# Expert thresholds found in two shares of sixteen experts, the second inside the loop of experts

## The reference, cut to what matters

```python
Sm = softmax(xf @ W_router + b_router)           # 8192 tokens x 32 experts
G_ek, idx_ek = jax.lax.top_k(Sm.T, 256)          # for each expert
tokens = xf[idx_ek]
up = einsum(tokens, W_up[group]) + b_up          # 128 -> 341, one W_up for 4 experts
Eout = einsum(silu(up), W_down[e]) + b_down      # 341 -> 128
y = zeros.at[idx_ek].add(G_ek[..., None] * Eout)
h = h + y
```

## Time and profile before

| what | value |
|---|---|
| median of 3 runs | 1282.54 us (1282.24 to 1286.24) |
| the profiled execution, its time | 1287.31 us |
| the profiled execution, its span | 1285.5 us |
| PE busy, DVE, ACT, POOL | 1072.1, 829.3, 677.6, 736.3 us |
| mean granted TensorE clock | 0.930 of full speed |
| chain that ended last: POOL, issue, PE, DVE, ACT | 8%, 7%, 4%, 2%, 1% |

### The profile page before, as it was taken

The page is one execution under the profiler, slowest core; times in us unless marked ns, Lnnn a source line. Parts: engine busy times, 40 slices in busy tenths (PEclk is TensorE's granted clock), DMA queues, the critical chain, the costliest instruction groups (busy, mean ns, idle before and its releaser), DMA issues. The chain is left out here.

```text
span 1285.5 us, 22999 instructions
## 1 busy us (share of the span) xinstructions
PE 1072.1 (83%) x7461; PEld 949.1 (74%) x7463; DVE 829.3 (65%) x2546; ACT 677.6 (53%) x1707; POOL 736.3 (57%) x1188
## 2 busy tenths in 40 slices
PE   3669999999999999999999999999992237757671
PEld 2558988988988998998899899898882125545451
DVE  5346677787877777787777778777775884422220
ACT  0335766666665666666566666666663543222220
POOL 5355675676467557646754764444443006788784
PEclk9979999999999999999999999999996558998886
DMA  3010010010001001000100100000002003444442
GB/s 101 18 32 20 18 30 24 18 36 20 26 24 34 24 10 39 25 25 24 34 24 9 40 24 26 12 9 19 12 9 77 0 4 67 80 84 75 83 68 23
DMA packets 49082, 42.60 MB, mean 33 GB/s; under 512 B 6728, under 2 KB 44488, under 8 KB 48840
## 3 DMA queue, kind: packets, MB, share of 16 engines
q0 software_dynamic: 18432, 22.04, 9.0%
q1 hardware_dynamic: 30536, 19.13, 4.8%
HBM read 27.51 MB, written 13.63 MB: 32 GB/s over the span
## 5 line engine op out<-in xcount | busy, mean ns | idle before, releaser
L634 PE MATMUL mixed<-v,pT 128*128 128x131 f32 x2560 | 320.1, 276 | 5.2 <-issue 4.5
L634 PEld LDWEIGHTS mixed<-v,pT 128*128 128x128 f32 x2560 | 302.9, 191 | 5.9 <-issue 5.6
L1100 POOL DMA_INDIRECT gram<-in_emb,ids x192 | 191.1, 995 | 71.6 <-issue 50.8
L871 DVE TENSOR_REDUCE neg_max<-scores 128x1 f32<-128x1024 f32 (+1 forms) x192 | 199.2, 1038 | 47.1 <-PE scores L437 46.2
L1028 ACT ACTIVATE probs<-scores,neg_max 128x1024 f32<-128x1024 f32 (+1 forms) x192 | 186.7, 972 | 33.7 <-DVE neg_max L871 31.7
L1037 ACT ACTIVATE pT<-turned 128x512 f32<-128x512 f32 x211 | 125.4, 595 | 63.7 <-PE turned L615 60.0
L1151 POOL TENSOR_TENSOR zb<-row,gate 128x384 f32<-128x384 f32 x64 | 54.7, 854 | 146.0 <-DVE gate L906 145.2
L435 PE MATMUL scores<-k_hi,q_hi 128*128 128x512 f32 x320 | 135.4, 423 | 2.3 <-issue 2.3
L615 PE MATMUL turned<-con,probs 128*128 128x128 f32 x844 | 124.8, 277 | 14.8 <-DVE h L793 4.8
L437 PE MATMUL scores<-k_hi,q_lo 128*128 128x512 f32 x320 | 126.7, 396 | 0.0
L436 PE MATMUL scores<-k_lo,q_hi 128*128 128x512 f32 x320 | 125.7, 393 | 0.0
(11 more groups left out here) (305 smaller groups left out, 2427.9 us busy)
## 6 DMA issues: line engine op xcount, KB each, us to landing
wd<-in_w_down SPq DMA_DIRECT2D x32, 171.0 KB
token_table<-w SPq DMA_DIRECT2D x16, 320.0 KB
out_h<-h SPq DMA_DIRECT2D x16, 256.0 KB, 2.3
gram<-in_emb,ids POOLq DMA_INDIRECT x192
wu<-in_w_up SPq DMA_DIRECT2D x8, 170.5 KB
w<-in_weights SPq DMA_DIRECT2D x1, 1174.0 KB
xg<-token_table,slots POOLq DMA_INDIRECT x64
out_h<-yw,slots POOLq DMA_INDIRECT x64
```

The lines of the kernel that those rows point to most:

```text
L634: last = pe.matmul(mixed[:, 0:C + 3], pT[:, n % 2, j * P:(j + 1) * P], vals[:, 0:C + 3], start=(j == 0), stop=(last_half and j == half * 4 ...
L871: dve.tensor_reduce(neg_max[:, n % 4:n % 4 + 1], scores[:, (n % 2) * S:(n % 2) * S + width], AX_X, ALU.max, negate=True).then_inc(maxed, 1)
L1100: pool.indirect_dma_start(gram[:, t % 4, g, :], None, emb[g], bass.IndirectOffsetOnAxis(ap=ids[:, s, t, g:g + 1], axis=0)).then_inc(gather ...
```

## The change

It makes two shares of 16 experts of the search. With 16 experts the 128 partitions are 16 experts x 8 chunks of 1024 tokens, so `probT` has two blocks of 1024 columns, one per share, and DVE counts 576 tokens of a partition and ACT 448 (`SPLIT` 1152 to 576). The first share is searched in 30 rounds ahead of everything, as before. The 30 rounds of the second share are put into iterations 0 to 9 of the loop, 2, 2, 4, 2, 4, 4, 2, 4, 3 and 3 of them (`ROUNDS`). In an iteration, the first round stands ahead of `up` on PE, the second ahead of `down`, the third and fourth behind `down`. On DVE the first two stand at the start; the count of the third stands ahead of `weigh`, the rest of it and the fourth behind. ACT counts in the places between. In the second share PE waits for DVE's count ahead of the first of its three matmuls. Groups 3 and 4, which need the thresholds of the second share, are chosen at e = 10 and 13 in place of 5 and 8; the second triple has three experts in place of two, and later triples are ranked at 11, 14, 16, 18, 21 and 24. A second copy of the low-bit-set values for ACT (`odd[:, 1, :]`, 448 columns) is made ahead of the loop. The transposes that make `probT`, and the last step of the router, write the same amounts in another order.

The core of the diff:

```diff
-CHUNKS = P // NE
-SPLIT = 1152
+SHARES = 2
+EH = NE // SHARES
+CHUNKS = P // EH
+SPLIT = 576
@@
-    TRIPLES = [range(0, 1), range(1, 3)] + [range(e, min(e + 3, NE)) for e in range(3, NE, 3)]
+    TRIPLES = [range(0, 1)] + [range(e, min(e + 3, NE)) for e in range(1, NE, 3)]
-    TRIPLE_AT = {3 * (g - FIRST_TRIPLES): g for g in range(FIRST_TRIPLES, len(TRIPLES))}
-    PLACE_BANK = (2, 3, 1, 1, 0)
-    IN_LOOP = {1: 2, 5: 3, 8: 4}
+    TRIPLE_AT = {0: 3, 3: 4, 6: 5, 11: 6, 14: 7, 16: 8, 18: 9, 21: 10, 24: 11}
+    PLACE_BANK = (2, 3, 1, 0, 1)
+    IN_LOOP = {1: 2, 10: 3, 13: 4}
+    ROUNDS = (2, 2, 4, 2, 4, 4, 2, 4, 3, 3)
+    def rounds_of(e):
+        return range(sum(ROUNDS[:e]), sum(ROUNDS[:e + 1]))
@@ PE
+        def total(h, k):
+            pe.wait_ge(cand_ok[h], k + 1)
+            if h > 0:
+                pe.wait_ge(counted[h], k + 1)
+            pe.matmul(total_at(h), fours[:], limits[:, 0:1], start=True, stop=False)
+            pe.wait_ge(counted_a[h], k + 1)
+            pe.matmul(total_at(h), less_one[:], count_a[:, h:h + 1], start=False, stop=False)
+            pe.wait_ge(counted[h], k + 1)
+            pe.matmul(total_at(h), less_two[:], count[:, h:h + 1], start=False, stop=True).then_inc(totalled[h], 1)
@@ PE, loop
                 rank(TRIPLE_AT[e])
+            totals(rounds_of(e)[0:1])
             if e + 1 < NE:
                 up(e + 1)
             if e in TRIPLE_AT:
                 rows_before(TRIPLE_AT[e])
             if e in IN_LOOP:
                 sums(IN_LOOP[e])
+            totals(rounds_of(e)[1:2])
             down(e)
+            totals(rounds_of(e)[2:])
@@ DVE
+        def count_bit(h, k, tokens):
+            dve.wait_ge(cand_ok[h], k + 1)
+            dve.tensor_scalar(below[:, 0:tokens], probT[:, h * HC:h * HC + tokens], cand[:, h:h + 1].bitcast(F32), None,
+                              ALU.is_lt, ALU.add, accum_out=count[:, h:h + 1]).then_inc(counted[h], 1)
+        dve.tensor_scalar(odd[:, 1, :].bitcast(I32), probT[:, HC + SPLIT:2 * HC].bitcast(I32), 1, None, ALU.bitwise_or
+                          ).then_inc(odd_later, 1)
         for e in range(NE):
+            for ks in (rounds_of(e)[0:1], rounds_of(e)[1:2]):
+                later_count(ks)
+                later_settle(ks)
+            last_rounds = rounds_of(e)[2:]
+            later_count(last_rounds[0:1])
             if e in TRIPLE_AT:
                 reach(TRIPLE_AT[e])
             weigh(e)
+            later_settle(last_rounds[0:1])
+            for k in last_rounds[1:]:
+                later_count([k])
+                later_settle([k])
@@ ACT, loop
+            later_count(rounds_of(e)[0:1])
             if e in TRIPLE_AT:
                 keep_ranks(TRIPLE_AT[e])
+            later_count(rounds_of(e)[1:2])
             if e + 1 < NE:
                 silu(e + 1)
             if e in IN_LOOP:
                 keep_sums(IN_LOOP[e])
+            later_count(rounds_of(e)[2:])
```

More of the change, by code:

```diff
@@ L553, in probT_item @@
             def probT_item(j, dst):
[L554 to L559, removed]
+                blocks = range(j * 2, min(j * 2 + 2, TT // CHUNKS - 1))
+                pe.wait_ge(route_v, (blocks[-1] + 1) * 10)
+                for h in range(SHARES):
+                    for i, u in enumerate(blocks):
+                        at = (h * len(blocks) + i) * P
+                        last = pe.transpose(dst[:, at:at + P],
+                                            prob[:, h, u * CHUNKS:(u + 1) * CHUNKS, :].rearrange("p c e -> p (c e)"), ident)
                 return last
@@ L1305, in experts @@
     odd_ok = sem("odd_ok")
[L1306 to L1310, removed]
+    odd_later = sem("odd_later")
+    counted = [sem(f"counted{h}") for h in range(SHARES)]
+    counted_a = [sem(f"counted_a{h}") for h in range(SHARES)]
+    totalled = [sem(f"totalled{h}") for h in range(SHARES)]
+    both_ok = [sem(f"both_ok{h}") for h in range(SHARES)]
+    cand_ok = [sem(f"cand_ok{h}") for h in range(SHARES)]
     thr_v = sem("thr_v")
@@ L1383, in triple_of @@
     def triple_of(e):
-        return e // 3 + 1 if e else 0
+        return (e + 2) // 3
     ctx.enter_context(nc.allow_low_precision(reason="counts are whole numbers of at most 2048, which float16 holds exactly"))
@@ L1411, in _ @@
     def _(pe):
-        pe.transpose(scores[:, 0:P], prob[:, (CT - 1) * CHUNKS:CT * CHUNKS, :].rearrange("p c e -> p (c e)"), ident
-                     ).then_inc(prob_turned, 1)
+        for h in range(SHARES):
+            last = pe.transpose(scores[:, h * P:(h + 1) * P],
+                                prob[:, h, (CT - 1) * CHUNKS:CT * CHUNKS, :].rearrange("p c e -> p (c e)"), ident)
+        last.then_inc(prob_turned, 1)
         pe.wait_ge(less_ok, 2)
         pe.wait_ge(limits_set, 2)
[L1418 to L1425, removed]
+        def total(h, k):
[7 more added lines that the diff above has]
+            pe.matmul(total_at(h), less_two[:], count[:, h:h + 1], start=False, stop=True).then_inc(totalled[h], 1)
@@ new lines, in total_last, with thresholds @@
+        def total_last(h):
+            pe.wait_ge(cand_ok[h], BITS)
+            pe.wait_ge(counted[h], BITS)
+            pe.matmul(total_at(h), fours[:], limits[:, 1:2], start=True, stop=False)
+            pe.matmul(total_at(h), less_one[:], count[:, h:h + 1], start=False, stop=True).then_inc(totalled[h], 1)
+        def thresholds(h):
+            pe.wait_ge(cand_ok[h], BITS + 1)
+            pe.transpose(thr_at(h), cand[0:EH, h:h + 1].bitcast(F32).to_broadcast([EH, P]), ident[0:EH, 0:EH]
+                         ).then_inc(thr_t, 1)
@@ L1427, in _, with totals @@
+        def totals(ks):
+            for k in ks:
+                if k < BITS - 1:
+                    total(1, k)
+                else:
+                    total_last(1)
+                    thresholds(1)
         with pe.Fori(0, (BITS - 1) // STEP) as g:
             for j in range(STEP):
-                total(g * STEP + j)
+                total(0, g * STEP + j)
         for k in range((BITS - 1) // STEP * STEP, BITS - 1):
-            total(k)
-        pe.wait_ge(cand_ok, BITS)
-        pe.matmul(turned[:, 0:1], fours[:], limits[:, 1:2], start=True, stop=False)
@@ L1434, in _ @@
[L1434 to L1438, removed]
+            total(0, k)
+        total_last(0)
+        thresholds(0)
         pe.wait_ge(made, 7)
@@ L1581, in _ @@
     def _(dve):
-        DONE = (CT - 1) * P
-        dve.memset(cand[:], 1 << (BITS - 1)).then_inc(cand_ok, 1)
-        dve.tensor_scalar(odd[:, 0:DONE - SPLIT].bitcast(I32), probT[:, SPLIT:DONE].bitcast(I32), 1, None, ALU.bitwise_or
+        DONE, HC = (CT - 1) * P, CT * P
+        for h in range(SHARES):
+            dve.memset(cand[:, h:h + 1], 1 << (BITS - 1)).then_inc(cand_ok[h], 1)
+        dve.tensor_scalar(odd[:, 0, 0:DONE - SPLIT].bitcast(I32), probT[:, SPLIT:DONE].bitcast(I32), 1, None, ALU.bitwise_or
                           ).then_inc(odd_ok, 1)
         dve.memset(fours[:], 4.0).then_inc(limits_set, 1)
-        for j, limit in enumerate((2 * (TOK - TOPK) - CHUNKS * (CT * P - SPLIT), TOK - TOPK)):
+        for j, limit in enumerate((2 * (TOK - TOPK) - CHUNKS * (HC - SPLIT), TOK - TOPK)):
             dve.memset(limits[0:NE, j:j + 1], limit / NE)
@@ L1592, in _ @@
         dve.wait_ge(prob_turned, 1)
-        dve.tensor_scalar(odd[:, DONE - SPLIT:].bitcast(I32), scores[:, 0:P].bitcast(I32), 1, None, ALU.bitwise_or
+        dve.tensor_scalar(odd[:, 0, DONE - SPLIT:].bitcast(I32), scores[:, 0:P].bitcast(I32), 1, None, ALU.bitwise_or
                           ).then_inc(odd_ok, 1)
         dve.wait_ge(bits_in, 32)
[L1597 to L1607, removed]
+        def count_bit(h, k, tokens):
+            dve.wait_ge(cand_ok[h], k + 1)
+            dve.tensor_scalar(below[:, 0:tokens], probT[:, h * HC:h * HC + tokens], cand[:, h:h + 1].bitcast(F32), None,
+                              ALU.is_lt, ALU.add, accum_out=count[:, h:h + 1]).then_inc(counted[h], 1)
@@ L1609, in _, with keep_thresholds, later_count, later_settle @@
+        def keep_thresholds(h):
+            dve.wait_ge(thr_t, h + 1)
+            dve.tensor_copy(thr[:, h * EH:(h + 1) * EH], thr_at(h)).then_inc(thr_v, 1)
+        def later_count(ks):
+            for k in ks:
+                count_bit(1, k, SPLIT if k < BITS - 1 else HC)
+        def later_settle(ks):
+            for k in ks:
+                settle_bit(1, k)
+                if k == BITS - 1:
+                    keep_thresholds(1)
         with dve.Fori(0, (BITS - 1) // STEP) as g:
             for j in range(STEP):
-                try_bit(g * STEP + j, SPLIT)
+                count_bit(0, g * STEP + j, SPLIT)
+                settle_bit(0, g * STEP + j)
@@ L1612, in _ @@
         for k in range((BITS - 1) // STEP * STEP, BITS - 1):
-            try_bit(k, SPLIT)
+            count_bit(0, k, SPLIT)
+            settle_bit(0, k)
         dve.wait_ge(prob_copied, 1)
[L1616 to L1620, removed]
+        count_bit(0, BITS - 1, HC)
```

(17 more changed lines are left out.)

40 lines of the change are left out of this document (29 added, 11 removed).

## The result

The changed kernel is **slower**: 1293.57 us median (1290.86 to 1295.13, 5 runs) against 1282.54 (1282.24 to 1286.24, also 5 runs), a ratio of 1.0078, interval 1.0059 to 1.0096, or +11.0 us between the medians. The prediction was 1275.7 with a range of 1267 to 1287. Direction, size and range were wrong.

What follows compares the result with a forecast made beforehand. It took the search rounds, then POOL's indirect DMAs from scatter 1 on, to bound the kernel. Terms -18.5 + 0.9 + 4.8 + 1.0 + 5.0 = -6.8 us took the 1282.5 median to 1275.7 us, range 1267 to 1287.

Steps and rivals of the forecast that it cites:

- The search: Search ahead of the loop: a round takes 1.42 us in place of 2.02, in sum -18.5 us.
- bit operation: Ahead of iteration 0 on DVE: the operation on 448 columns for ACT's second copy adds 0.4 us.
- What a round costs in an iteration: Loop iterations 0 to 9: two rounds add 1.25 us, three 1.65, four 3.3; scatter 9 +4.8 us.
- The clock: First ten iterations: PE at the lower clock a third of the time, as in a later stretch, +5 us.
- my sum at full clock: Scatter of expert 9 stands 73.1 us behind the copy ahead of iteration 0, where it stood at 68.3.
- The base: Scatter 9 before the change at 68.3 us, from a profiled execution 4.8 us above the median.
- Behind scatter 9: Loop from iteration 10 on: POOL bounds it again; late results and comparisons beside POOL add 1.0 us (0 to 3).
- The first, full clock throughout: Loop: PE's clock stays at full speed, -11.8 us, 1270.7 us; chance 0.17.
- The second, low clock throughout: Loop: clock low nearly throughout, up to 13 us more than taken, 1280 to 1289 us; chance 0.13.
- The third, rounds that don't overlap: Loop: rounds don't overlap with the expert, 1.62 us each, scatter 9 at 98, in sum 1295 us; chance 0.10.
- The fourth: Loop: DVE's counts hold up POOL's indirect DMAs, scatter 9 at 90 us, time 1287 us; chance 0.04.
- The fifth: Loop: change costs nothing there, POOL stays the bound with a fourth round hidden, -16.6, 1266 us; chance 0.06.

## Why the prediction was wrong, by its own steps

**The search: right.** 2.02 to 1.43 us a round, and from the first count to the copy ahead of iteration 0 it is 62.6 us where it was 79.8: -17.2, where the sum had -18.5 + 0.9 = -17.6 (bit operation counted apart).

**What a round costs in an iteration: right.** At full clock four rounds make 7.18 to 7.26 us (7.24), a triple with two 7.0 (7.1), three rounds 5.55 (5.6), in the kernel with columns where PE waits and in the one iteration with single columns at full clock. That up comes 1.0 us late, that the second round hides under up but for 0.25, and that the fourth is uncovered, is to be seen in the rows above.

**The clock: this step failed.** I took a later stretch of the kernel before, 0.83, as the nearest row, and a third of the time at the lower level: +5 us. Measured is 0.57 over iterations 2 to 8:

```profile
1064.00:1132.00 68.00, 49.71 (x235) 37.05 (x235) 38.04 (x166) 28.10 (x82) 36.03 (x28) 0.57 0.30 54
```

Scatter 9 stands 91.0 - 73.1 = 17.9 us behind my sum at full clock, where I took 5: **12.9 us** of the miss. The upper end that I gave, 18 us for half clock throughout, is what came, though in part by luck: its price per iteration was too low and its count of iterations at half clock too high. The row was the wrong neighbour. In that later stretch PE waits once, for gathered rows, and then does the work of an expert in one go; in the changed loop it waits ahead of up and again behind down, and between that wait and the next it has, in a plain iteration, only three matmuls of one column and the transposes. Four more of these in each round left the clock at 0.63, and four of 256 columns gave 0.94. Why the clock falls under the one pattern and less under the other no run here separates further. Where it has fallen, the iteration is 10.3 us for 7.2. Nor was the price per iteration right: 2.3 us by the earlier trace rows, where `down` of 2.49 had run partly at full clock; at half clock throughout it is 2.91, and the iteration 3.0 to 3.1 longer. The 73.1 is itself no pure sum at full clock: the 8.33 us that I took for iteration 1 stand at a clock of 0.80, and at 1.00 it is 6.98, in the kernel before with columns. So the clock's whole cost to scatter 9, changed kernel against the one with columns where PE waits, is 91.0 - 71.8 = 19.2 us.

**The base: 2.2 us.** The sum set the change against scatter 9 at 68.3 in one execution 4.8 us above its median; near the median it is 66.0. I had noted the 4.8 and took it off again as if it lay elsewhere.

**Behind scatter 9: 1.1 us.** From there to the end it is 1292.0 - 1139.3 = 152.7 us and was 150.0; +2.7, less the 0.6 by which the execution before nearest to the median differs (150.6), where I had 1.0. Scatter 10 comes 8.7 us behind scatter 9: POOL waits 2.11 us for DVE's result in iteration 10, which chooses a group and has a clock of 0.65. Scatter 13 comes 8.0 behind 12, by a slow instruction and a landing (first scatter instruction of experts 12 and 13):

```profile
1161.02 2.42 POOL L1919 DMA_INDIRECT out_h<-yw,slots  x1 [0.30 <-issue]
...
1169.00 1.62 POOL L1919 DMA_INDIRECT out_h<-yw,slots  x1 [1.07 <-DMA out_h<-yw,slots]
```

The comparisons of `find_over` and `find_ties` stand beside the first, at 1160.1 to 1162.0. In the kernel before the same pair, 2.46 and a wait of 1.05, stood ahead of scatter 7. This term is the least sure: in the traces of kernels with rounds in the loop the stretch takes 149.2 to 153.0 us.

In sum 12.9 + 2.2 + 1.1 + 0.4 for the search make 16.6 of the 17.8 us between -6.8 and +11.0; the rest is within what two medians tell (the interval is +7.6 to +12.3 us).

**The rivals.** The first, full clock throughout, at -11.8 us, is what the kernel with columns where PE waits comes near: 0.9924 of 1282.5 is -9.7. The second, low clock throughout, was right in mechanism and in the 13 us that it added, and I gave it 0.13 and a time of at most 1289, since the base was wrong too. The third, rounds that don't overlap, fell by the periods at full clock. The fourth fell: beside counts, POOL's scatter instructions take 1.57 to 1.63 us as before; a slow one (2.02) stands beside the comparisons at 1139.9 to 1141.8. The Trainium skill, page SBUF — State Buffer, section Who interferes with whom, says that a DVE instruction with at most one SBUF input, outside the 2-port modes, does not contend with GpSimd, and the traces agree. The fifth fell, since a fourth round is not hidden.

The wait for the count that PE has ahead of the first matmul of a round in the second share costs the 0.20 us that the kernel with both searches ahead shows. No run here takes it away in the loop.

## What to carry to other kernels

Before moving a latency-bound chain of small steps into a loop that has room, ask what PE's clock will be there: cost the loop at full and at half clock, and if the lower one exceeds the room, count it as likely where PE is to wait several times in each iteration, as here. A handful of wide matmuls into an unused part of a bank, put only where PE waits, kept the clock up and turned +0.8% into -0.8%; put where PE does not wait, they cost their own length (8.6 us an iteration for 7.2). And set the sum against an execution near the median, or read two traces of it.

## What the runs showed of the hardware that I had not expected

- With the three matmuls of one column in a round, and four more of one column beside them, the clock fell (0.63 over iterations 2 to 8); with four of 256 columns it stood at 0.81 to 1.00 in each of these iterations.
- Three matmuls of 256 columns in every 1.43 us of the search did not raise the clock from 0.50 in 37 us, and four in every 2.03 us did not either. In the loop, with up and down between them, such matmuls kept the clock up; in the search, with other operands and nothing else but single columns, they did not lift it. Which of these differences matters, no run here tells.
